# Linear attention in pieces of 64 tokens, with the denominators turned before the second score burst, and rounding of a mixture on another engine

## What is computed

```python
x = x + y                                   # y: causal convolution, then w_pw
q, k, v = split(einsum(x, w_qkv))           # 16 heads of 8
q_phi, k_phi = elu(rope(q)) + 1, elu(rope(k)) + 1
kv_prefix = cumsum(k_phi[..., :, None] * v[..., None, :], axis=1)
k_prefix  = cumsum(k_phi, axis=1)
num   = einsum('bthd,bthdm->bthm', q_phi, kv_prefix)
denom = sum(q_phi * k_prefix, axis=-1)
x = x + sigmoid(gate(delta)) * ((num / (denom + 1e-6)) @ w_o.T)
h = layernorm(x)
x = x + sum_e softmax(h @ w_moe_gate.T)[e] * (silu(h @ w1[e].T + b1[e]) @ w2[e].T + b2[e])
```

## Time and profile before

| | us |
|---|---|
| median of 3 runs | 1476.04 |
| lowest and highest of them | 1470.7, 1478.65 |
| the profiled execution | 1480.5 |
| its span, first to last instruction | 1478.7 |
| PE, DVE, ACT, POOL busy in it | 1266.4, 1013.0, 814.8, 712.6 |
| mean granted clock of PE | 0.925 |

### The profile page before, as it was taken

How to read it: one execution, slowest core, us unless ns; L and a number is a source line. 1 busy time by engine, 2 the same in 40 slices (tenths; PEclk the granted TensorE clock), 3 DMA queues, 4 the chain that set the end, 5 groups by cost and what they waited for, 6 DMA issues and landing times. The chain is left out here.

```text
span 1478.7 us, 33273 instructions
## 1 busy us (share of the span) xinstructions
PE 1266.4 (86%) x10164; PEld 984.0 (67%) x10164; DVE 1013.0 (69%) x3390; ACT 814.8 (55%) x1703; POOL 712.6 (48%) x907
## 2 busy tenths in 40 slices
PE   2899999999986999999999965883988888739998
PEld 1566767676655877777777754773666666539997
DVE  3588888888735899999999984764566666522222
ACT  2355555556426776767777643552556555525554
POOL 3355565656420234343443542335566676426666
PEclk9799999999877999999999986996999999859999
DMA  1101011110102321212112205674111112168872
GB/s 62 40 30 39 31 33 33 31 37 28 45 13 62 69 54 44 64 41 62 40 48 59 73 16 142 196 202 146 27 44 47 49 55 44 44 233 300 266 264 69
DMA packets 70844, 117.53 MB, mean 79 GB/s; under 512 B 9746, under 2 KB 36635, under 8 KB 70768
## 3 DMA queue, kind: packets, MB, share of 16 engines
q1 hardware_dynamic: 58736, 93.49, 21.3%
q0 software_dynamic: 9856, 21.52, 4.6%
q10 hardware_dynamic: 2176, 1.61, 0.4%
HBM read 79.35 MB, written 29.88 MB: 74 GB/s over the span
## 5 line engine op out<-in xcount | busy, mean ns | idle before, releaser
L1159 DVE TENSOR_TENSOR m_Sl<-m_S,m_Sh 128x512 fp32r<-128x512 f32 x256 | 195.5, 769 | 23.3 <-ACT m_S L1076 20.6
L1076 ACT ACTIVATE m_S<-PS,W 128x512 f32<-128x512 f32 x256 | 174.7, 690 | 39.0 <-issue 33.1
L1071 ACT ACTIVATE m_Sh<-PS,W 128x512 fp32r<-128x512 f32 x192 | 132.9, 692 | 72.1 <-PE PS L996 64.5
L1459 POOL DMA_INDIRECT rows<-r_row,r_posi x128 | 131.2, 1025 | 36.2 <-issue 36.0
L761 DVE TENSOR_TENSOR am<-PS,C 128x512 f32<-128x512 f32 x192 | 119.6, 678 | 25.9 <-PE PS L454 25.4
L1693 PEld LDWEIGHTS PS<-f_wt,f_hid 128*128 128x128 f32 x960 | 121.3, 194 | 4.4
L1693 PE MATMUL PS<-f_wt,f_hid 128*128 128x128 f32 x960 | 121.5, 277 | 0.0
L1682 PE MATMUL PS<-f_xT,f_wt 128*128 128x256 f32 x480 | 121.2, 390 | 0.0
L965 POOL TENSOR_TENSOR m_oe<-m_oe 128x512 f32<-128x512 f32 x48 | 67.8, 1412 | 102.2 <-DVE m_oe L1140 101.7
L994 PE MATMUL PS<-m_HH,m_w1h 128*128 128x512 f32 x256 | 107.7, 421 | 7.1 <-DVE m_w1l L1112 4.7
L352 POOL TENSOR_TENSOR am<-am,C 128x512 f32<-128x512 f32 x64 | 81.6, 1275 | 54.8 <-ACT am L636 53.5
(11 more groups left out here) (237 smaller groups left out, 3127.2 us busy)
## 6 DMA issues: line engine op xcount, KB each, us to landing
f_wt<-wr SPq DMA_DIRECT2D x40, 578.0 KB
f_row<-rows SPq DMA_DIRECT2D x40, 260.0 KB
f_wt<-wr SPq DMA_DIRECT2D x40, 256.0 KB, 2.8
m_gb<-gates SPq DMA_DIRECT2D x8, 1024.0 KB, 7.7
m_raw<-gates SPq DMA_DIRECT2D x8, 1024.0 KB, 7.9
f_row<-rows SPq DMA_DIRECT2D x40, 132.0 KB, 2.1
mid<-f_res SPq DMA_DIRECT2D x20, 256.0 KB, 3.3
X<-x SPq DMA_DIRECT2D x16, 256.0 KB, 2.8
```

Source lines behind the costliest of these rows:

```text
L1071: nc.scalar.activation(Sh[:, n % 4, :], PS[:, n % 3, :], ACT.Silu, bias=w("b1")[:, n:n + 1]).then_inc(sh_ready, 1)
L1076: nc.scalar.activation(S[:, n % 3, :], PS[:, n % 3, :], ACT.Silu, bias=w("b1")[:, n:n + 1]).then_inc(s_ready, 1)
L1159: nc.vector.tensor_tensor(Sl[:, n % 4, :], S[:, n % 3, :], Sh[:, n % 4, :].bitcast(F32), ALU.subtract).then_inc(sl_ready, 1)
L1459: nc.gpsimd.indirect_dma_start(out=self.rows, out_offset=bass.IndirectOffsetOnAxis(ap=self.posi[:, u, t:t + 1], axis=0), in_=self.row[:, u ...
```

## The change

A piece becomes 64 tokens, of which a batch has 8. Scores come in two bursts instead of four, p = 0 and 1, with two old tiles each; a product has 64 columns and its output is 64 partitions, so that two stand beside each other in a row tile. A bank holds eight triangles of 64 by 64, so the masks work on as many elements as before, but there are 6 on DVE, 2 copies on ACT and 2 masks on POOL in place of 12, 4 and 4. The state is no longer built up in a bank. `chunks(f)` makes the seven k'v products of the next batch in one go, DVE masks them in two instructions (`mask_chunks`), and POOL adds them up one after another (`add_chunks`). `weigh` has a state product, `carried_over`, in front of each of its groups j. The outputs go to banks 5 and 6, and `divide` reads both. `turn_k` and `copy_k` now come in the stage before the one that uses them. `turn_spread` and `copy_rdT` move from the end of the stage to ahead of the second score burst. In the mixture, `ROUNDED` is empty: ACT makes Sh for all chunks, and DVE casts none.

```diff
 HEADS, HD = 16, 8
+HALF = P // 2
+PAIRS = CT // 2
...
+            def add_chunks(b, first, end):
+
+                pool.wait_ge(chunks_read, 2 * b + 2)
+                for k in range(first, end):
+                    if k > 1:
+                        pool.wait_ge(state_ready, STATES * b + k - 1)
+                    here = state[:, k % 2, k // 2, :]
+                    nc.gpsimd.tensor_tensor(here, here, state[:, (k - 1) % 2, (k - 1) // 2, :], ALU.add).then_inc(state_ready, 1)
...
+                if b is not None:
+                    add_chunks(b, 1, 3)
                 if f is not None:
                     sum_rotated(f, 0)
-                    differences(f, u, c_)
+                if b is not None:
+                    add_chunks(b, 3, 5)
+                    mask_last(b, 0)
+                if f is not None:
                     sum_rotated(f, 1)
                 if b is not None:
-                    mask_last(b, 0)
+                    add_chunks(b, 5, 7)
+                if f is not None:
+                    differences(f, u, c_)
+                if b is not None:
                     keep_x1(b, u)
                     mask_last(b, 1)
                 if c_ is not None:
                     inverse_deviation(c_, ln2_stats, mv2, ve2, ve2_done, rstd2, rstd2_ready, shift2, shift2_ready, z_ready, negated2)
-                if b is not None:
-                    mask_last(b, 2)
                 if f is not None:
                     weigh_keys(f, u)
-                if b is not None:
-                    mask_last(b, 3)
...
             def turn_k(b, u):
 
                 pe.wait_ge(phi_ready, 2 * b + 2)
-                for t in range(CT - 1):
-                    mm = nc.tensor.transpose(PS[:, 6, (t + 1) * P:(t + 2) * P], kphi[:, u, t * P:(t + 1) * P], ident)
+                after_previous(pe, raw_ready, b, PAIRS)
+                for t in range(CT):
+                    mm = nc.tensor.transpose(PS[:, 4, t * P:(t + 1) * P], kphi[:, u, t * P:(t + 1) * P], ident)
...
+            def chunks(b, u):
+
+                pe.wait_ge(ktok_ready, b + 1)
+                after_previous(pe, am_ready, b, 6)
+                for k in range(2 * CT - 1):
+                    t, rows = k // 2, slice(HALF * (k % 2), HALF * (k % 2) + HALF)
+                    mm = nc.tensor.matmul(PS[:, 2 + k % 2, t * P:(t + 1) * P], ktok[rows, t, :], vt[rows, u, t, :],
+                                          start=True, stop=True)
+                mm.then_inc(chunks_psum, 1)
...
-                for g in range(4):
-                    for j in range(4):
-                        rows, cols = slice(32 * j, 32 * j + HD), slice(t * P, (t + 1) * P)
-                        mm = nc.tensor.matmul(PS[:, 1 + j, g * P:(g + 1) * P], kr[rows, u, g, cols], qr[rows, u, g, cols],
-                                              start=True, stop=True)
-                        if g == 3:
-                            mm.then_inc(scores_psum, 1)
...
+                for t in (2 * p, 2 * p + 1):
+                    for g in range(4):
+                        at = (t % 2 * 4 + g) * HALF
+                        for j in range(4):
+                            rows = slice(32 * j, 32 * j + HD)
+                            for half in range(2):
+                                cols = slice(t * P + half * HALF, t * P + half * HALF + HALF)
+                                mm = nc.tensor.matmul(PS[half * HALF:half * HALF + HALF, 1 + j, at:at + HALF],
+                                                      kr[rows, u, g, cols], qr[rows, u, g, cols], start=True, stop=True)
+                            if t % 2 and g == 3:
+                                mm.then_inc(scores_psum, 1)
+
+            def weigh(b, u, p):
+
+                def carried_over(k, first=0, end=HALF):
+
+                    t, half = k // 2, k % 2
+                    cols = slice(t * P + half * HALF + first, t * P + half * HALF + end)
+                    return nc.tensor.matmul(PS[:, 5 + half, t * HALF + first:t * HALF + end],
+                                            state[:, (k - 1) % 2, (k - 1) // 2, :], qphi[:, u, cols],
+                                            start=False, stop=False, skip_group_check=True)
+
+                if p == 0:
                     pe.wait_ge(den_step, 2 * b + 1)
                 else:
-                    pe.wait_ge(ktok_ready, b + 1)
-                nc.tensor.matmul(PS[:, 6, 0:P], ktok[:, t, :], vt[:, u, t, :], start=(t == 0), stop=True,
-                                 skip_group_check=True).then_inc(state_psum, 1)
-
-            def weigh(b, u, t):
-
-                if t == 0:
-                    after_previous(pe, attn_ready, b)
-                else:
-                    pe.wait_ge(state_ready, 3 * b + t)
-                    nc.tensor.matmul(PS[:, 5, t * P:(t + 1) * P], state[:, t - 1, :],
-                                     qphi[:, u, t * P:(t + 1) * P], start=True, stop=False, skip_group_check=True)
+                    pe.wait_ge(state_ready, STATES * b + STATES)
                 for j in range(4):
+                    if p == 0 and j in (1, 2):
+                        pe.wait_ge(state_ready, STATES * b + j)
                     if j == 3:
-                        pe.wait_ge(last_ready, 4 * b + t + 1)
+                        pe.wait_ge(last_ready, PAIRS * b + p + 1)
                     else:
-                        pe.wait_ge(am_ready, 12 * b + 3 * t + j + 1)
-                    for g in range(4):
-                        mm = nc.tensor.matmul(PS[32 * g:32 * g + 32, 5, t * P:(t + 1) * P],
-                                              vm[:, u, t, j, 32 * g:32 * g + 32],
-                                              am[:, j, g * P:(g + 1) * P],
-                                              start=(t == 0 and j == 0), stop=(j == 3), skip_group_check=True)
+                        pe.wait_ge(am_ready, 6 * b + 3 * p + j + 1)
+                    if p:
+                        carried_over(4 + j)
+                    elif j < 2:
+                        carried_over(1 + j)
+                    else:
+                        carried_over(3, (j - 2) * HALF // 2, (j - 1) * HALF // 2)
+                    for t in (2 * p, 2 * p + 1):
+                        for g in range(4):
+                            at = (t % 2 * 4 + g) * HALF
+                            for half in range(2):
+                                rows = slice(half * HALF, half * HALF + HALF)
+                                mm = nc.tensor.matmul(PS[32 * g:32 * g + 32, 5 + half, t * HALF:t * HALF + HALF],
+                                                      vm[rows, u, t, j, 32 * g:32 * g + 32], am[rows, j, at:at + HALF],
+                                                      start=(t == 0 and j == 0 and half == 0), stop=(j == 3), skip_group_check=True)
                     mm.then_inc(am_used, 1)
 
...
@@ -533,44 +575,38 @@
                 mm.then_inc(lg_psum, 1)
 
             def steps(b, u, n, f, c_):
-                if b is not None:
-                    turn_k(b, u)
                 if c_ is not None:
                     gate(c_, 1 - u)
                 if b is not None:
                     scores(b, u, 0, f)
+                    denominators(b)
                 if c_ is not None:
                     project_out(c_)
                 if f is not None:
                     values(f, 1 - u)
                 if b is not None:
-                    update_state(b, u, 0)
                     weigh(b, u, 0)
-                    scores(b, u, 1, f)
-                    denominators(b)
                 if n is not None:
                     turn_xn(n)
+                if b is not None:
+                    turn_spread(b)
+                    scores(b, u, 1, f)
                 if c_ is not None:
-                    turn_x2(c_)
-                if b is not None:
-                    update_state(b, u, 1)
-                    weigh(b, u, 1)
-                    scores(b, u, 2, f)
+                    turn_x2(c_, b)
                 if n is not None:
                     pointwise(n)
                 if b is not None:
-                    update_state(b, u, 2)
-                    weigh(b, u, 2)
-                    scores(b, u, 3, f)
-                if c_ is not None:
-                    turn_z(c_)
+                    weigh(b, u, 1)
+                if f is not None:
+                    turn_k(f, 1 - u)
                 if n is not None:
                     project(n, u, "q", 0)
                 if c_ is not None:
+                    turn_z(c_)
+                if f is not None:
+                    chunks(f, 1 - u)
+                if c_ is not None:
                     logits(c_)
-                if b is not None:
-                    weigh(b, u, 3)
-                    turn_spread(b)
                 if n is not None:
                     project(n, u, "k", 1)
             stages(pe, steps)
@@ -615,7 +651,7 @@
...
```

(35 more changed lines are left out.)

92 lines of the change are left out of this document (45 added, 47 removed).

## The result

The changed kernel took 1559.68 us (median of 4 runs, 1552.68 to 1563.13) where the kernel before took 1473.37 on the same chip. The ratio is 1.0582, 95% interval 1.0522 to 1.0642: slower by 86 us. The profiled execution took 1561.2 us. I had forecast 1495, at most 1535: the direction was right, the size was not.

The account below looks back on a forecast made before the run. PE was taken to bound the kernel, DVE close behind; after the change a chain of waits (25.5 us a stage, 26.7 with the clock). 1480.5 + 36 (front) - 17 (mixture) = 1499.5 profiled, so 1495 us median; range 1466 to 1535.

Parts of the forecast that it names:

- Direction: Whole kernel: the change makes it slower, chance 0.70, against 0.14 for faster and 0.16 for the same.
- Chain: Attention front: a loop of waits through DVE, POOL, ACT and PE sets the stage, 25.5 us at full clock.
- The wait before turn_z: End of a front stage: PE waits 1.5 us for ACT's z, as copy_k stands ahead of normalise2.
- The clock: Front: more stretches at 1.2 GHz add 1.2 us a stage, between 0 and 3, to the 25.5.
- Small products: PE in the front: eight run side by side, a score burst 1.1 us, a weighing group 0.75 us.
- C1: Rival, front: small products run four side by side, not eight, plus 23 us, 1518 us; chance 0.07.
- C2: Rival, front: small instructions are fed no faster than 34 ns each, plus 88 us, 1583 us; chance 0.06.
- Mixture: Mixture: fewer DVE casts give back PE's waiting behind DVE, minus 17 us, bounds 0 and minus 25.
- the wait for s_ready grows only a little: Mixture: ACT keeps up with PE's chunks, with 3 banks ahead; 0.2 us was taken off for ACT.
- the 1.3 us a batch: Mixture: PE's waits behind DVE and the weight reloading behind each, which can come back, some 1.3 us a batch.
- Rival E: Mixture gives nothing back, as ACT's longer turn delays s_ready as much as DVE's shortens; 1512 us, chance 0.12.
- D: Rival, front: chain isn't closed, PE stays the bound, stage 22.7 us, 1443 us; decides from 24.6 us downward; chance 0.13.

Follow-up runs that it names:

- e3: Changed kernel with its order and waits, but half the score and weighing products (odd halves left out); ratio 1.056, stage 30.67 us.
- e11: e3 with 12 useless transposes before the first weighing only; ratio 1.027, stage 27.23 us.
- e10: e3 with useless transposes before turn_z (10) and logits (4) only; ratio 1.057, stage 30.70 us.
- e15: Kernel before, with DVE's phi(f, 0) ahead of the first score masks, so PE waits before the first weighing; ratio 1.026, stage 26.66 us.
- e2: Kernel before, with four stages in PE's front loop body in place of two; ratio 1.011, stage 24.83 us.
- e7: Changed kernel with useless transposes before turn_z (10), logits (4) and the first weighing (12); ratio 1.041, stage 28.82 us.
- e8: e3 with the useless transposes of e7 at the same three places; ratio 1.030, stage 27.24 us.
- e4: e3 with four stages in PE's loop body, as in e2; ratio 1.060, stage 29.18 us.
- e16: e3 with DVE's invert ahead of phi(f, 0), taking away the wait before the first weighing; ratio 1.055, stage 29.46 us.
- e18: e16 with ACT's copy of k behind normalise2 and 12 useless transposes before the first weighing; ratio 1.020, stage 26.38 us.

## Why the prediction was wrong

- **Direction: right. Chain: right in e3, and its agreement in the changed kernel in part luck.** From DVE's chunk mask to turn_xn the working has 3.4 + 5.7 + 3.8 = 12.9 us, and e3 12.8 (though PE gets there just as late by the denominators and the first weighing, which the working had as a wait only). From there e11 has 9.3 for 8.5 (200.35 to 209.68), 2.25 for 2.3 and 1.8 for 1.8: 26.2 us for 25.5 at full clock. The wait before turn_z came at its place, with 1.23 us for 1.5; H's is 0.45. The 1.3 us of signals in the sum are my estimate and stand on no row. In the changed kernel ACT's copy of k starts 0.04 us after the last transpose of k has ended (222.95), which is 0.21 after the start of PE's next line (222.78), from where the working counts; PE's transposes of z start 0.05 us after ACT's last z has ended (224.98, 225.03; ACT's rows below). In the changed kernel PE waits for v in 3 of 11 stages and for the denominators in 2, so the loop through DVE, POOL and ACT is not what bounds most stages: waits on other engines are 24.0 us in 11, 2.2 a stage for my 4 to 5, and "issue" is another 1.7. That 25.2, itself only a lower bound, is near 25.5 rests on both. POOL's state sums took some 0.49 us, inside 0.3 to 0.6.

```profile
222.99 0.60 ACT L676 ACTIVATE ktok<-PS 128x512 f32<-128x512 f32 x1 [2.79 <-PE PS L453]
223.48 1.50 ACT L647 ACTIVATE z<-PS,shift,rstd 128x128 f32<-128x128 f32 x4
```

- **The clock: the step that failed.** "I take 1.2 us on top of the 25.5, between 0 and 3." It was half of 11.8, 5.9 us at most (31.17 less 25.2), and 4.5 in e3 by the 26.2 us just summed (30.67 less 26.2). Over the 13 stages that I counted, the 4.7 us missing are 61 us, of the 65 by which the forecast was short. I took the row of one 3.4 us stretch in two stages and put "one such stretch in every stage and a second in some" for it. The rows gave no reason for a bound of 3: they showed what PE did before a fall, small products with hardly a wait (busy in 3.27 of 3.40 us), and I knew that the change would double the number of bursts' products and add four waits. Shown: with the same order and the same full-clock stage, dense work at one place takes some 7 us of low clock and 3.47 us of the stage away (e10, e11); and waits of 1.2 us a stage put into the kernel before cost 2.7 us, 1.7 of them by the clock (e15). That the time is lost at the low clock is shown; why the clock falls is open, as waits, stops for fetches and small products are not separated, and no run has the small products in the old order.
- **Small products: half right.** Weighing groups took 0.74 us for 0.75 (205.35 to 206.09), as the sum for eight side by side has it, and C1 falls for them. The first score burst took 1.52 us at full clock, between the 1.1 of eight and the 2.0 of four. The second one is the one on the chain, with 0.95 in the sum: some 2.5 us with a stop for "issue" in it, and 1.94 in e3. So this term was 1.0 to 1.5 us short, and not by the 34 ns an instruction of C2, as 1.52 us are 12 ns. Why a score burst takes longer than summed is open; in e3 half as many products of the same columns, with 128 output partitions in place of 64, took longer still. The 0.20 us for two changes of shape stand in the trace of before at the ends of a burst: the second four start 0.21 us after the first four (196.15, 196.36), the next line 0.22 after the last four (197.03, 197.25), and the fours between follow each other at 0.11. What the array does in that time no row shows.
- **Instruction fetches: missing from the sum.** PE's instruction queue went from 36 packets to 103. "Issue" is 18.7 us of the 43 us idle in 11 stages, and three of the five stops where the loop turns stand ahead of 6.8 to 10.2 us at 1.2 GHz, so part of the clock term may be theirs. What it costs in the end isn't settled: e2 says 0.86 us a stage in the kernel before (11 us over 13 stages, 16 by the ratio); e7 against e8 1.6 us, in which the count of products differs too; e4 against e3 nothing.
- **Mixture: right, a size off.** 11.6 us for 17, inside its bounds of 0 and 25. PE's waits behind DVE are gone, as forecast, but "the wait for s_ready grows only a little" was wrong: it went from 1.3 to 6.8 us in 230 us of the mixture (600 to 830 before, 700 to 930 after). Nor do the 1.3 us a batch come out of their terms: 7.9 us over 8.8 batches are 0.9, twice that is 1.8. For the reloading the trace of before has less: the first product behind a wait takes 0.50 us where the median is 0.39 (L1011), and 0.33 where it is 0.27 (L1488), 0.17 us a batch. Rival E falls. D falls too: the stage at full clock alone is above its 24.6.

```profile
PE PS L994 <- ACT m_S L1076: 1.3, 8, 0.2
```

```profile
PE PS L1026 <- ACT m_S L1108: 6.8, 9, 0.8
```

- **Size of the waits.** No wait of PE in e3 was over 1.3 us, and its clock fell once in every stage. That the idle times alone do it isn't borne out, as e16 is without the longest of them and its clock is no higher (0.81 for 0.83).

## What to carry to other kernels

Where a stage already has one stretch at the low clock, price a change's added waits and thinner products at twice their own length or more (2.3 times the waits put in, and 2.7 times the idle time added, in e15, the one case here), and let the range reach to a stage with two fifths of its time at 1.2 GHz, as was seen here. Test for it cheaply: useless dense matmuls in front of a wait, and if the kernel gets faster, the clock was holding it back. Try more than one place, as one gave everything here and the other nothing (e11, e10). And count the instructions of a loop body before unrolling it or splitting its products.

## What the runs showed of the hardware

- A kernel got 3.4 us a stage faster by 12 transposes whose result nobody reads (e3 to e11), and in e18 such work (1.3 us) left the stage as it was, 26.38 for 26.47 us, where PE waited for nothing at that place.
- The clock's ups and downs can repeat with the pipeline: 10.24 us at 1.2 GHz and 20.48 at 2.4 in every stage of e3.
- A loop body of some 1300 or 1400 PE instructions with the weight loads (before, e3) goes with 36 packets on the instruction queue in the whole run; bodies of some 2400 and 2600 (after, e2) with 103 and 67, and with stops where the loop turns.
- A score burst of 128 instructions with 64 columns in and 64 out partitions took 1.52 us at full clock, one of 64 with 128 output partitions 1.94 (231.81 to 233.75 below, e3): half as many products took longer.

```profile
231.81 2.01 PE L484 MATMUL PS<-qr,kr 8*128 8x64 f32 x64 [0.31 <-issue]
233.75 1.06 PE L530 MATMUL PS<-C,prod 128*128 128x16 f32 x8
```
